# Flamingo block on one core: once normed rows and the context's norm to ScalarE, the context's scale and offset in eight wide products

## What is computed

```python
def _layernorm(x, g, b):                  # without g, b: the plain one
    m = mean(x); v = mean((x - m) ** 2)
    return (x - m) * rsqrt(v + EPS) * g + b

z    = ctx @ W_in + b_in
zn   = _layernorm(z, g_ln, beta_ln)       # the context's norm
h    = silu(pe @ Wp1 + bp1) @ Wp2 + bp2
conv = irfft(rfft(window * h) * rfft(zn)) # a causal convolution over time
x1   = layernorm(x)                       # the "once normed" rows
y    = silu(_layernorm(x1, g1, be1) @ W1a + b1a) @ W1b + b1b + x1
y    = y * conv[:, idx]
y    = silu(_layernorm(y, g2, be2) @ W2a + b2a) @ W2b + b2b + y
x    = x + tanh(g_xattn) * y
x    = x + tanh(g_ffn) * moe(layernorm(x))  # 16 experts, best 2 of them
```

## Time and profile before

| | us |
|---|---|
| median of 3 runs | 887.68 |
| lowest, highest | 887.09, 892.47 |
| the profiled execution | 882.99 |
| its span, first to last instruction | 881.2 |
| TensorE busy | 808.5 (92%) |
| VectorE busy | 530.5 (60%) |
| ScalarE busy | 671.0 (76%) |
| GpSimd busy | 512.8 (58%) |

### The profile page before, as it was taken

The page is one execution under the profiler, slowest core; times in us unless marked ns, Lnnn a source line. Parts: engine busy times, 40 slices in busy tenths (PEclk is TensorE's granted clock), DMA queues, the critical chain, the costliest instruction groups (busy, mean ns, idle before and its releaser), DMA issues.

```text
span 881.2 us, 23828 instructions
## 1 busy us (share of the span) xinstructions
PE 808.5 (92%) x9954; PEld 386.4 (44%) x9954; DVE 530.5 (60%) x963; ACT 671.0 (76%) x841; POOL 512.8 (58%) x392
## 2 busy tenths in 40 slices
PE   7987999787699898779989999999999999999996
PEld 2654566555455555423324343433343433334433
DVE  2999866553557576546636666566566565664443
ACT  3333555444567754369999999999999999999994
POOL 1162622324546452117748878778678787787675
PEclk9997999899999988889989999999999999999999
DMA  7790299961023221166535555555545555555551
GB/s 277 153 238 26 70 175 206 194 129 30 27 63 79 61 60 36 49 160 176 138 96 155 155 164 150 157 162 156 164 146 169 154 159 152 163 157 152 155 156 46
DMA packets 85027, 117.09 MB, mean 133 GB/s; under 512 B 13076, under 2 KB 65428, under 8 KB 84693
## 3 DMA queue, kind: packets, MB, share of 16 engines
q1 hardware_dynamic: 84920, 115.58, 50.5%
HBM read 101.32 MB, written 6.94 MB: 123 GB/s over the span
## 4 chain that ended last, share of the span: by engine, by line
PE 69%; ACT 12%; DVE 11%; POOL 4%; issue 3%; DMA 0%; POOLq 0%; ACTq 0%; SPq 0%; DVEq 0%
PE PB L720 22%; PE PA L708 15%; PE PT L708 8%; ACT WK L1358 7%; PE PB L531 7%; PE PA L514 4%; PE PB L730 2%; POOL WK L1391 2%; PE PB L571 2%; PE PA L475 2%; PE PT L607 1%; DVE SM L790 1%; PE PB L460 1%; DVE DC L900 1%; POOL SM L1385 1%
## 5 line engine op out<-in xcount | busy, mean ns | idle before, releaser
L1447 POOL TENSOR_TENSOR WK<-WK 128x512 f32<-128x512 f32 x240 | 322.6, 1344 | 121.9 <-DVE WK L1170 112.4
L1358 ACT ACTIVATE WK<-PA 128x1024 f32<-128x1024 f32 x342 | 356.3, 1163 | 2.3 <-PE PA L708 1.6
L720 PE MATMUL PB<-WK,EW 128*32 128x512 f32 x2048 | 265.7, 594 | 0.5 <-ACT WK L1358 0.5
L708 PE MATMUL PA<-RA,EW 98*32 98x512 f16 x2736 | 199.0, 381 | 5.0 <-ACT WK L1358 5.0
L1358 ACT ACTIVATE WK<-PT 128x1024 f32<-128x1024 f32 x170 | 197.5, 1161 | 3.8 <-PE PT L708 3.5
L1391 POOL TENSOR_TENSOR WK<-WK 128x512 f16<-128x512 f32 x64 | 94.4, 1493 | 114.0 <-ACT WK L1233 112.9
L708 PEld LDWEIGHTS PA<-RA,EW 98*32 98x32 f16 x2736 | 66.5, 95 | 156.9 <-issue 71.9
L708 PE MATMUL PT<-RA,EW 98*32 98x512 f16 x1360 | 103.7, 381 | 1.5 <-DVE DC L866 1.5
L1385 POOL TENSOR_TENSOR SM<-SM 128x4 f32<-128x4 f32 (+1 forms) x24 | 30.1, 1254 | 115.8 <-DVE SM L829 73.8
L720 PEld LDWEIGHTS PB<-WK,EW 128*32 128x32 f32 x2048 | 62.1, 111 | 54.4 <-DVE WK L1170 1.7
L1230 ACT ACTIVATE WK<-PA,CV 128x512 f16<-128x512 f32 x64 | 44.0, 687 | 48.3 <-PE PA L514 47.3
(11 more groups left out here) (176 smaller groups left out, 1091.4 us busy)
## 6 DMA issues: line engine op xcount, KB each, us to landing
RA<-wpd SPq DMA_DIRECT2D x128, 134.1 KB, 5.6
W1h<-wtd SPq DMA_DIRECT2D x128, 128.0 KB, 2.7
DC<-wtd SPq DMA_DIRECT2D x128, 128.0 KB, 2.8
W2h<-wtd SPq DMA_DIRECT2D x128, 128.0 KB, 2.7
W2l<-wtd SPq DMA_DIRECT2D x128, 128.0 KB, 2.7
WK<-in_x SPq DMA_DIRECT2D x16, 512.0 KB, 3.9
RA<-DC SPq DMA_DIRECT2D x96, 64.0 KB, 2.0
out<-WK SPq DMA_DIRECT2D x16, 256.0 KB, 2.8
```

Source lines behind the costliest of these rows:

```text
L708: m = pe.matmul(PRE[k % 3][32 * j:32 * j + 32, 512 * q:512 * q + 512], EW1[0:98, 128 * e + 32 * j:128 * e + 32 * j + 32], TS[0:98, h, 512 ...
L720: m = pe.matmul(o[32 * q:32 * q + 32, :], EW2[:, 32 * e:32 * e + 32], hb[:, 512 * q:512 * q + 512], start=True, stop=True)
L1358: ac.activation(HB[n % NH][:, 1024 * p:1024 * p + 1024], PRE[k % 3], ACT.Gelu, scale=1.0 / SC).then_inc(a_gelu, 1)
L1447: po_.tensor_tensor(AC[g], AC[g], PR[m % 3], ALU.add).then_inc(g_ac, 1)
```

## The change

- **Once normed rows.** ScalarE makes them (`normed_once`: four activations, scale 1/sigma, bias -mean/sigma). VectorE makes only the bias, 4 columns (`once_shift`, semaphore `v_x1`). `v_x0` becomes `a_x0`. The loads of x wait for `v_nm` and `a_x0`. On ScalarE, tile 0's stand behind W1's high half and ahead of the silu of tile 0, tile 1's behind that silu, and tile s + 1's in stage s ahead of the silu of tile s.
- **Turned rows' low halves.** `turn_lo(1)` moves ahead of the context's statistics.
- **The context's norm.** ScalarE makes (z - mean)/sigma with sixteen activations of 256 columns (`context_normed`, eight in s = 2 and eight in s = 3, ahead of the silu). VectorE makes the bias of these (`context_shift`). Then VectorE multiplies by g_ln and adds beta_ln in pairs of 1024 columns (`context_affine(0)` in s = 2, 1 to 3 in s = 3).
- **Order.** The context's statistics 1 and 2 are made in s = 1 behind `first_norm(2)`, number 3 behind `first_out(0)` with the aggregate. The split of zn4 (`context_hi`, `context_lo`) moves from s = 3 to s = 4. GpSimd makes the context's power behind `layer1_lo(1)`.

```diff
@@ sync
-            sp.wait_ge(v_x0, 1)
+            sp.wait_ge(v_nm, 1)
+            sp.wait_ge(a_x0, 1)
             load_x(0, 2)
...
-                    sp.wait_ge(v_x0, s + 1)
+                    sp.wait_ge(v_nm, s + 1)
+                    sp.wait_ge(a_x0, s + 1)
                     load_x(0, s + 2)
@@ vector
-            def normed_once(b):
+            def once_shift(b):
+
                 o = 160 + 48 * (b % 3)
-                if b == 2:
-                    ve.wait_ge(v_br, 1)
-                apply(XS[b % 2], XN0[b % 3], SM[:, o + 24:o + 32], SM[:, o + 32:o + 36], v_x0)
+                ve.wait_ge(g_pow, b + 1)
+                ve.scalar_tensor_tensor(out=SM[:, o + 40:o + 44], in0=SM[:, o + 24:o + 32:2], scalar=-1.0, in1=SM[:, o + 32:o + 36],
+                                        op0=ALU.mult, op1=ALU.mult).then_inc(v_x1, 1)
...
+            def context_shift():
+
                 ve.wait_ge(g_zpow, 1)
...
+                ve.scalar_tensor_tensor(out=zsh, in0=zmv[:, 0:32:2], scalar=-1.0, in1=zr, op0=ALU.mult, op1=ALU.mult).then_inc(v_zs, 1)
+
+            def context_affine(p):
+
+                x = zf[:, 1024 * p:1024 * p + 1024]
+                ve.wait_ge(a_zn, p // 2 + 1)
+                ve.tensor_tensor(x.rearrange("p (b n) -> p b n", b=4), x.rearrange("p (b n) -> p b n", b=4),
+                                 row(R_GLN).unsqueeze(1).broadcast_to([128, 4, 256]), ALU.mult).then_inc(v_zg, 1)
+                ve.wait_ge(v_zg, p + 1)
+                ve.tensor_tensor(zn4[:, :, :, 4 * p:4 * p + 4].rearrange("p s j b -> p b j s"),
+                                 x.rearrange("p (b j s) -> p b j s", b=4, s=2),
+                                 row(R_BLN).rearrange("p (j s) -> p j s", s=2).unsqueeze(1).broadcast_to([128, 4, 128, 2]),
+                                 ALU.add).then_inc(v_zb, 1)
...
-            normed_once(1)
-            for p in range(1, 4):
-                context_stats(p)
...
+            once_shift(1)
+            turn_lo(1)
             for s in range(1, NB + 1):
                 if s + 1 < NB:
                     first_norm(s + 1)
                 if s == NB:
                     break
-                if s < 5:
+                if 1 < s < 5:
                     turn_lo(s)
+                if s == 1:
+                    context_stats(1)
+                    context_stats(2)
+                if s == 2:
+                    context_shift()
                 if s == 3:
                     layer1_bias(1, PA[:, 1024:1028])
+                if s == 4:
+                    context_lo(0)
+                    context_lo(1)
                 if s + 1 < NB:
+                    once_shift(s + 1)
                     normed_twice(s + 1)
-                    normed_once(s + 1)
-                if s == 1:
-                    context_scaled(0)
-                if s == 2:
-                    context_offset(0)
+                if s == 3:
+                    context_affine(1)
...
                 if s == 2:
-                    context_offset(1)
+                    context_affine(0)
                 if s == 3:
-                    for u in range(4):
-                        context_lo(u)
+                    context_affine(2)
+                    context_affine(3)
+                if s == 4:
+                    context_lo(2)
+                    context_lo(3)
@@ scalar
+            def normed_once(b):
+
+                o = 160 + 48 * (b % 3)
+                ac.wait_ge(v_x1, b + 1)
...
+                for t in range(4):
+                    a = ac.activation(XN0[b % 3][:, 256 * t:256 * t + 256], XS[b % 2][:, 256 * t:256 * t + 256], ACT.Identity,
+                                      scale=SM[:, o + 32 + t:o + 33 + t], bias=SM[:, o + 40 + t:o + 41 + t])
+                a.then_inc(a_x0, 1)
+
+            def context_normed(u):
+                ac.wait_ge(v_zs, 1)
+                for bb in range(8 * u, 8 * u + 8):
+                    x = zf[:, 256 * bb:256 * bb + 256]
+                    a = ac.activation(x, x, ACT.Identity, scale=zr[:, bb:bb + 1], bias=zsh[:, bb:bb + 1])
+                a.then_inc(a_zn, 1)
...
             split_hi(XR[:, 1024:2048], W1["h"][:, 1024:2048], a_w1h)
+            normed_once(0)
             ac.wait_ge(v_be, 1)
             layer1(0, C_B1A)
+            normed_once(1)
...
             for s in range(1, NB):
                 if s < 5:
                     turn(s)
-                if s == 3:
+                if s == 4:
                     for u in range(4):
                         context_hi(u)
+                if s + 1 < NB:
+                    normed_once(s + 1)
+                if s in (2, 3):
+                    context_normed(s - 2)
@@ gpsimd
             power(2)
+            layer1_lo(1)
             po_.wait_ge(v_zep, 1)
             po_.tensor_tensor(zr, zr, SM[:, 6:7].broadcast_to([128, 16]), ALU.pow).then_inc(g_zpow, 1)
-            layer1_lo(1)
```

More of the change, by code:

```diff
@@ L155, in flamingo_kernel @@
         zf = DC[:, 4096:8192]
-        zst, zmv, zr = SM[:, 16:112], SM[:, 112:144], SM[:, 144:160]
+        zst, zmv, zr, zsh = SM[:, 16:112], SM[:, 112:144], SM[:, 144:160], SM[:, 304:320]
         zn4 = DC[:, 0:4096].rearrange("p (s j b) -> p s j b", s=2, b=16)
@@ L252, in flamingo_kernel @@
         v_zst, v_zag, v_zep, v_zg, v_zb = (sem("v_" + n) for n in ("zst", "zag", "zep", "zg", "zb"))
-        v_zl, v_dc, v_x0 = (sem("v_" + n) for n in ("zl", "dc", "x0"))
+        v_zl, v_dc, v_x1, v_zs = (sem("v_" + n) for n in ("zl", "dc", "x1", "zs"))
         v_rv, v_br, v_w2l, v_wm, v_wo, v_eb, v_ew = (sem("v_" + n) for n in ("rv", "br", "w2l", "wm", "wo", "eb", "ew"))
@@ L923, in conv_out @@
                 ve.wait_ge(p_flip, c + 1)
+                if c == 0:
+                    ve.wait_ge(v_zl, 4)
                 ve.tensor_reduce(DC4[:, :, CH * c:CH * c + CH, :], f, AX.X, ALU.add).then_inc(v_dc, 1)
@@ L1063, in vector_program @@
             ve.tensor_tensor(BR[32:33, :], RVS[32:33, :], BR[32:33, :], ALU.subtract).then_inc(v_br, 1)
-            normed_once(1)
-            for p in range(1, 4):
-                context_stats(p)
-            ve.wait_ge(v_zst, 4)
-            for bb in range(16):
-                a = ve.bn_aggr(zmv[:, 2 * bb:2 * bb + 2], zst[:, 6 * bb:6 * bb + 6])
-            a.then_inc(v_zag, 1)
-            ve.wait_ge(v_zag, 1)
-            ve.tensor_scalar(zr, zmv[:, 1:32:2], EPS, None, ALU.add).then_inc(v_zep, 1)
+            once_shift(1)
+            turn_lo(1)
             for s in range(1, NB + 1):
@@ L1106, in vector_program @@
                 if s == 1:
-                    context_scaled(1)
+                    context_stats(3)
+                    ve.wait_ge(v_zst, 4)
+                    for bb in range(16):
+                        a = ve.bn_aggr(zmv[:, 2 * bb:2 * bb + 2], zst[:, 6 * bb:6 * bb + 6])
+                    a.then_inc(v_zag, 1)
+                    ve.wait_ge(v_zag, 1)
+                    ve.tensor_scalar(zr, zmv[:, 1:32:2], EPS, None, ALU.add).then_inc(v_zep, 1)
                 if s == 2:
-                    context_offset(1)
+                    context_affine(0)
                 if s == 3:
-                    for u in range(4):
-                        context_lo(u)
+                    context_affine(2)
[3 more added lines that the diff above has]
+                    context_lo(3)
                 for c in chunks(s):
@@ L1255, in normed @@
                 a.then_inc(done, 1)
+            def normed_once(b):
+                o = 160 + 48 * (b % 3)
+                ac.wait_ge(v_x1, b + 1)
+                if b == 2:
+                    ac.wait_ge(v_br, 1)
+                if b >= 3:
+                    ac.wait_ge(v_out, b - 2)
+                for t in range(4):
[8 more added lines that the diff above has]
+                a.then_inc(a_zn, 1)
             def gated_norm(b):
```

25 lines of the change are left out of this document (6 added, 19 removed).

## The result

| | before | changed |
|---|---|---|
| median of 20 runs, us | 886.45 | 894.35 |
| lowest, highest | 880.5, 892.8 | 890.62, 900.25 |
| profiled execution, its span | 882.99, 881.2 | 900.25, 898.4 |

A forecast was written before the change was run, and what follows sets the result against it. The chain was 69% TensorE; between 27 and 155 us TensorE stands still where feed-forward stages' inputs are late. 5 + 1.2 + 0.4 = 6.6 us on 882.99 gave 889.6, as a median 894.3; range 882 to 902.

The forecast's parts named there:

- First and second: Stage s = 1: layer 1 of tile 1 gains 4.3 us plus some 1.5; giving back leaves 2 to 4 us lead.
- Third: SyncE's queue moves 3.6 us; x tile 3 lands at 69.6, VectorE stands from 59.0, layer 1 of tile 2 2.3 late.
- rival 1: The stream catches up and x tile 3 lands at 66.0: +3.0 us, 890.7; chance 0.15.
- Fourth and fifth: s = 2 and context products: tile 2's silu waits until 79.8, layer 2 ends about 93; a wide pair takes 3.1 us.
- Sixth: s = 4: silu of tile 4 at 109.3 to 111.9, sums 4 us late, clock loss 1: together +5 us.
- Seventh: Later stages: s = 5 costs +1.2 us, s = 6 +0.4 us, s = 7 nothing.
- the rule of the Trainium skill about the lock: Lock between GpSimd and two-SBUF-input VectorE instructions: GpSimd's first low half of tile 3 held until 101, s = 4 at +5.3.
- Rival 2: Not slower: lead of s = 1 kept if x tile 3 lands before 59.0: -6.3 us, 881.4; chance 0.10.

The follow-up runs named there:

- the context back on VectorE: Changed kernel with VectorE scaling and offsetting the context again, its split back in s = 3; once normed rows stay on ScalarE: 885.24 us, ratio 0.9990.
- the swaps apart: Changed kernel with only the first context swap ahead of the tap loads of s = 4, the others behind pieces 1, 3 and 5: 892.01 us, ratio 1.0075.
- half taps: Second half of each piece's taps left out from piece 7 on: kernel before 879.04 us, ratio 0.9925; changed kernel 886.83 us, ratio 0.9997.
- x tile 3 first: Changed kernel with SyncE loading x tile 3 ahead of the six weights instead of behind them: 888.15 us, ratio 1.0022.
- with the swaps apart too: Changed kernel with x tile 3 loaded ahead of the six weights and three swaps moved behind tap loads of s = 4: 884.34 us, ratio 0.9996.
- EW1 split early: EW1 split in s = 4 and 5, not 6: alone on kernel before 888.02 us, 0.9998; with context, x tile 3 and swap edits on changed kernel 888.15, 1.0013.

## Why the prediction was right

The forecast was 894.3 us as a median, slower by 6.6 us against the profiled execution; measured are 894.35 and, as a difference of medians, 7.9. The hit in the median is closer than the working behind it deserves: 887.68 of three runs was the base, 886.45 of twenty is the better one. And a cost that the prediction left at nothing, the swaps, is in the trace. By its steps:

- **First and second (won in s = 1, given back).** Right to within 0.3 us: low halves until 49.2 (predicted 49.0), ScalarE's once normed rows done at 55.9 (55.8), the silu of tile 1 at 55.87.
- **Third (SyncE, x tile 3).** The wait came as described, and it matters: moving this load alone gives back 6 us. But it costs only with the context's work behind it (see the context back on VectorE). Its size was 2.5 us too large: the first load went out at 32.63 as worked out (32.5), but the queue caught up, 18.34 us for the 28 loads against 19.14 (the same queue took 19.06 in the run with the swaps apart) and less for the weights, so x tile 3 was issued at 56.06 (57.8) and VectorE went on at 67.13 (69.6). It stood for 7.62 us and not for 10.6. The low halves of tile 2 were done at 70.4, as before (70.7), so layer 1 of tile 2 was not 2.3 us late. On this point rival 1 (landing at 66.0) came nearer than the forecast; its time, 890.7, did not.
- **Fourth and fifth.** The silu of tile 2 began at 77.08 (79.8, the 2.5 us of the third step); the normed context took 4.0 us for eight (4.1). A pair took 3.2 us alone (3.1 taken) and 4.9 beside GpSimd (up to 5.5).
- **Sixth (s = 4).** The shift of tile 5 came at 106.45 (106.1 to 108.7), the silu of tile 4 at 109.65, within 109.3 to 111.9; first sums 3.0 us late, within 2.7 to 5.3, 4 taken. The clock loss was put at 1 of 0 to 2.5; the windows show a fall (to 0.70 in the profile, an estimate of at most 1.7 us; to 0.50 with half taps).
- **Seventh.** From the first sums to the first silu of the next stage the changed kernel lost another 2.4 us (5.4 against 3.0), where 1.2 was worked out for s = 5; the clock is the likely rest, which no run took by itself. For s = 6 it said 0.4; the profile shows 6.7 more, of which 4.0 are the wait for taps.
- **What the prediction left out.** The swaps. The change moves `context_lo` from s = 3 to s = 4, and the eight swaps that wait for it stand ahead of the taps of s = 4 in SyncE's queue. The prediction followed SyncE's queue for the first edit and not for this one, and counted nothing for it. The trace shows 7.0 us of delay of the taps and a DMA wait of 4.0 us in s = 5; that this makes the profiled execution so long, and whether a typical one has it, is not shown. Holding the taps alone costs 7 to 8 us. That the forecast came out right all the same is luck in part: the two delays run beside each other and don't add. With half of the taps left out, where the stream no longer fills the stages, the change costs 6 to 8 us as well, and with the swaps apart 0.75%.

On the rule of the Trainium skill about the lock (SBUF — State Buffer, "Who interferes with whom"): the wide pair beside GpSimd took 2.15 + 2.77 where it takes 1.23 + 1.95 alone, and GpSimd's four low halves 8.52 us where four take 4.61:

```profile
57.19 4.61 POOL L1429 TENSOR_TENSOR WK<-WK 128x512 f16<-128x512 f32 x4 [4.29 <-ACT WK L1245]
...
94.45 8.52 POOL L1429 TENSOR_TENSOR WK<-WK 128x512 f16<-128x512 f32 x4 [8.39 <-ACT WK L1245]
```

Both lost: GpSimd's first low half took 2.6 us (94.45 to 97.0), so the 5.62 us of the earlier trace rows did not come back. A lock per instruction allows both patterns, GpSimd kept waiting through four instructions of VectorE or the two taking turns; these rows do not tell what decides between them. First sums 3.0 us late lie near the lower end (2.7), not at the upper one (5.3) that the prediction worked out for a GpSimd kept waiting until 101.

Rival 2, the lead kept, asked for x tile 3 before 59.0. The run that gives it just that (x tile 3 first) has 6 us less than the changed kernel, not the 13 that the rival counted on; with the swaps apart too it is 8 by the ratios. The lead at s = 4 did not reach the end in any run.

## What to carry to other kernels

When an edit moves an instruction, follow each semaphore that it raises into the queues of DMAs, and ask what stands behind the waiting DMA there: here one load of 512 KB and eight swaps held what the next stages needed. Where two paths of nearly one length run side by side, mending one may show nothing, and a start earlier than both may be worth nothing either; experiments have to ease them singly and together before one of them is called harmless. An idle engine (here ScalarE) is no free place: what is put ahead of its urgent work inherits all the waits of what feeds it.

## What was not expected of the hardware

- A stretch with the DMA engines full cost time beyond the waits that are named for it. Halving the taps won 7.4 us of the kernel before (886.45 to 879.04, ratio 0.9925, 0.9895 to 0.9954), whose trace names no wait of TensorE for a tap. It has a stall of 1.85 us in the middle of a piece of the convolution, which the profile gives to nothing ("issue"), and which is not there with half taps:

```profile
185.41 0.30 PE L557 MATMUL PT<-RA 60*32 60x256 f16 x7
187.57 0.59 PE L557 MATMUL PT<-RA 60*32 60x256 f16 x25 [1.85 <-issue]
```

  The same stall, cut after 7 matmuls too, is in the changed kernel at 195.9 (2.07 us), in ten of the twelve profiles with full taps in all (1.2 to 2.9 us), and in neither with half taps; the two others, with EW1 split early, wait for taps there. That it is TensorE's own instructions coming late is a guess that no run here tests. The Trainium skill (Runtime: NRT & Kernel Launch, "Instruction fetch mechanics") says that a sequencer fetches its instructions by a DMA queue of its own.
- The same first matmuls take different times in different executions. Eleven f32 matmuls of 512 columns near the start, in the kernel before and in the one with the context on VectorE (timelines of TensorE):

```profile
11.36 9.53 PE L460 MATMUL PB<-RA 128*128 128x512 f32 x11
```

```profile
11.33 6.57 PE L464 MATMUL PB<-RA 128*128 128x512 f32 x11
```

  The changed kernel has 9.62 us. The granted clock is 1.00 in all three from 9 to 21 us. Five profiles have the short form (6.6 to 7.3 us), nine the long one (9.1 to 9.6); it is the 2 to 3 us by which the positions of the five are ahead. The change doesn't touch these matmuls, both forms come with and without it, and the profiles with the short form are no shorter as a whole, so the table leaves it out by counting from the silu of tile 0. Its cause is open.
- What stays open: what holds the silu of tile 7 at 154 to 155 us in all kernels whose both paths start by 72, and where the rest of the 7.4 us of the halved taps lies (the two profiles differ by 2.7 us there, and as whole executions by only 0.6, since the one of before is among the shortest of its runs and the one with half taps among the longest). Waits for taps and a lower clock are in these traces; no run took the clock by itself.
